# Exponentials of a score tile made per PSUM bank, and the product with V in bank order

## The chip, the cores and the metric

The kernel runs on one core of one Trainium2 chip. The time is that of one execution on the device, in microseconds (us); the median of several runs is compared. The engines are TensorE (PE in the profile, its weight loads PEld), VectorE (DVE), ScalarE (ACT), GpSimd (POOL) and SyncE (SP), which issues most transfers.

## The reference

A batch of 32 sequences of 128 tokens with 144 channels passes three transformer layers and then a rotation. Each layer is: normalise, modulate with a shift and a scale that come from a condition, attention with 16 heads of 9 channels, add; normalise, modulate, a multilayer perceptron (dense in layers 0 and 2, four experts with the best two chosen in layer 1), add. All in float32. The part that matters here is attention:

```python
scores = jnp.einsum('blhd,bmhd->bhlm', q * scale, k)
attn = jax.nn.softmax(scores, axis=-1)
o = jnp.einsum('bhlm,bmhd->blhd', attn, v).reshape(b, l, c)
return o @ W_proj + b_proj
```

The rotation at the end projects on 64 directions and applies a matrix exponential per sequence; its preparation runs on GpSimd, and in layer 1 on TensorE between other work (L1549).

## The kernel before

Each engine has its own instruction stream, written out by hand; they meet only through semaphores. A stream is in program order, so what stands where in the code is what the engine does next. Three layers follow each other, each with an attention stage and a perceptron stage. The attention stage is software-pipelined over pairs of sequences: the function `pair(i)` exists once per engine and interleaves steps of pairs i + 2 to i - 2.

For each sequence `b` there are two halves `a` of eight heads each. A half goes like this:

- `scores` on TensorE (L1375 and L1382). The product is made twice: with queries on the rows into `PSA`, from which VectorE takes the row maxima (L529), and with keys on the rows into `PSB`, with the maximum already subtracted. `PSA` and `PSB` are each two PSUM banks of 128x512 float32. Bank `r` of `PSB` is `PS[2 + r]` and holds four heads, one for each group `g` of 0 to 3.
- `exps` on ScalarE (L1070): one exponential over both banks of `PSB`, 128x1024, into `PT` in SBUF. `PT` is a part of the tensor BIG, so the profile writes BIG<-PSB. It adds 1 to the semaphore `exp_done`.
- `pv` on TensorE (L1399): eight products of `VA` (values of a head, and a column of ones that gives the sum of the row) with `PT`, into the one bank `PS[6]`. Each product writes 32 partitions, `p0 = HP * (2 * (g % 2) + r)` with HP = 32. The start partition decides which of the four 32-column tiles of the array works, so g and r pick the tile. A float32 product that isn't a transpose stands as two MATMUL and two LDWEIGHTS records in the trace.
- `out_copy` on ScalarE (L1076) copies `PS[6]` out, TensorE turns it back (`out_back`, L1419), VectorE divides by the sums (L541, L546), TensorE turns it again (`out_turn`, L1424 and L1425), and `project` (L1429, L1430) multiplies with the output weights.

Other names in the rows: `qk_turned` (L1360) transposes Q and K, and `qk_copy` on ScalarE (L1060) brings them to SBUF; `qkv_high` (L1046, L1047) and `qk_double` (L1053) prepare them; `max_turn` (L1411) transposes the maxima and `max_row` on VectorE (L537) adds them to Q; `h_modulate` (L1019, L1021) and `h_high` (L1033, L1034) prepare the normalised input; `split_product` (L1318) is the projection to Q, K, V and the first product of the perceptron, L1573 its second one.

The order around the change is set by hand in `pair`: ScalarE has for each pair `exps` for the odd sequence of the pair before (a = 1, then a = 0) and for the even one of this pair; TensorE takes the `pv` of these a half pair to a pair later. `scores` for the next half waits until `exps` has read `PSB`, by the same semaphore.

Of the kernel before, what the change touches and what calls it, by code (L numbers as in the profile page):

```python
# [8 lines left out]
ACT = mybir.ActivationFunctionType  # L9
AX = mybir.AxisListType  # L10

NB, T, C = 32, 128, 144
NH, HD = 16, 9
# [5 lines left out]
G, HG, HP = 4, 4, 32  # L19
# [28 lines left out]
def wait(eng, sem, value):  # L48

    if isinstance(value, int) and value <= 0:  # L50
        return
    eng.wait_ge(sem, value)
# [7 lines left out]
def program(nc, d, out, gates_dram, skew_dram):  # L60
    ctx = ExitStack()
    with ctx:
        def sb(name, shape, dt=F32):
            return ctx.enter_context(nc.sbuf_tensor(name, shape, dt))

        def sem(name):
            return ctx.enter_context(nc.semaphore(name))
# [22 lines left out]
        b2 = sb("b2", [128, NE, C])  # L90
# [18 lines left out]
        PT = BIG[:, 0:4096].rearrange("p (b a n) -> p b a n", b=2, a=2)  # L109
# [45 lines left out]
        PSA, PSB = (ctx.enter_context(nc.psum_tensor(f"PS{n}", [128, 1024], F32)) for n in ("A", "B"))  # L155
        PS = [PSA[:, 0:512], PSA[:, 512:1024], PSB[:, 0:512], PSB[:, 512:1024]]
# [21 lines left out]
        s2_done, exp_done = sem("s2_done"), sem("exp_done")  # L178
# [46 lines left out]
        def n_unit(l):  # L225
            return sum(EXPERTS[:l]) * NM
# [729 lines left out]
        def _(act):  # L956
            S = nc.scalar
# [52 lines left out]
            def attention(l):  # L1010
# [52 lines left out]
                def exps(b, u, a):  # L1063
                    act.wait_ge(s2_done, 2 * (NB * l + b) + 2 - a)
                    if b == 0:
                        wait(act, f2_done, n_unit(l) * MT)
                    if l == 1 and b == 0:
                        act.wait_ge(sk_st, 64)
                    wait(act, pv_done, NB * l + b - 1)
                    S.activation(PT[:, u % 2, a, :], PSB[:, :], ACT.Exp, scale=float(HD) ** -0.5).then_inc(exp_done, 1)  # L1070

                def out_copy(b, u):
                    n = NB * l + b
# [11 lines left out]
                def pair(i, gelus=None, high=None, rest=None):  # L1085
# [14 lines left out]
                    if last:  # L1100
                        exps(o - 2, o % 2, 1)
# [11 lines left out]
                    if last:  # L1113
                        exps(o - 2, o % 2, 0)
# [9 lines left out]
                    if at(0):  # L1124
                        exps(e, e % 2, 1)
# [142 lines left out]
        def _(pe):  # L1268
# [52 lines left out]
            def attention(l):  # L1321
# [42 lines left out]
                def scores(b1, b2, a):  # L1364

                    if b1 is not None:
                        wait(pe, max_done, 2 * (NB * l + b1) + a)
                    if b2 is not None:
                        pe.wait_ge(mrow, NB * l + b2 + 1)
                        wait(pe, exp_done, 2 * (NB * l + b2) + a)  # L1370
                    for g in range(G):
                        for r in range(2):
                            if b1 is not None:
                                rows, q0, par = slice(HP * (2 * a + r), HP * (2 * a + r + 1)), (b1 % 2) * 128, b1 // 2 % 2
                                one = mm(PS[r][:, g * 128:(g + 1) * 128], Q[rows, par, g, q0:q0 + 128],  # L1375
                                         KK[rows, par, g, q0:q0 + 128], start=True, stop=True)
                                if g == G - 1 and r == 1:
                                    one.then_inc(s1_done, 1)
                            if b2 is not None:
                                c = 1 - a  # L1380
                                rows, q0, par = slice(HP * (2 * c + r), HP * (2 * c + r + 1)), (b2 % 2) * 128, b2 // 2 % 2
                                two = mm(PS[2 + r][:, g * 128:(g + 1) * 128], KK[rows, par, g, q0:q0 + 128],  # L1382
                                         Q[rows, par, g, q0:q0 + 128], start=True, stop=True)
                                if g == G - 1 and r == 1:
                                    two.then_inc(s2_done, 1)

                def pv(b, u, a):

                    n = NB * l + b
                    if n == 0:  # L1390
                        pe.wait_ge(s_gev, 1)
                    if a == 1:
                        wait(pe, ot_ev, n)
                        pe.wait_ge(v_ev, n + 1)
                    pe.wait_ge(exp_done, 2 * n + 2 - a)
                    for g in range(G):
                        for r in range(2):
                            p0, at = HP * (2 * (g % 2) + r), (2 * a + g // 2) * 128
                            last = mm(PS[6][p0:p0 + HP, at:at + 128], VA[:, u, G * g + 2 * a + r, :],  # L1399
                                      PT[:, u % 2, a, (G * r + g) * 128:(G * r + g + 1) * 128], start=True, stop=True)  # L1400
                    if a == 0:
                        last.then_inc(pv_done, 1)
# [29 lines left out]
                def pair(i, first=None, turn_rows=None):  # L1432
# [7 lines left out]
                    if at(1):  # L1440
                        pv(e - 2, (e - 2) % 4, 1)
                    if at(2):
                        out_turn(e - 4, e % 2)
                    if now:
                        pe.wait_ge(qk_rd, 4 * (NP * l + i) + 2)
                    scores(e if now else None, o - 2 if before else None, 0)
                    if at(1):
                        pv(e - 2, (e - 2) % 4, 0)
# [8 lines left out]
                    if now:  # L1457
                        qk_turned(i, 3)
                    scores(e if now else None, o - 2 if before else None, 1)
                    if at(-1):  # L1460
                        qkv_product(i + 1, 0)
# [4 lines left out]
                    if before:  # L1466
                        pv(o - 2, (o - 2) % 4, 1)
# [9 lines left out]
                    if now:  # L1477
                        pe.wait_ge(qk_rd, 4 * (NP * l + i + 1))
                        scores(o, e, 0)
# [446 lines left out]
```

## Time and profile before

| | |
|---|---|
| median of three runs | 1349.75 us |
| lowest, highest | 1345.43, 1353.05 us |
| the profiled execution | 1347.33 us |
| its span, first to last instruction | 1345.5 us |
| granted TensorE clock, mean | 0.975 of full |
| TensorE busy | 1233.1 us, 92% |
| VectorE busy | 916.0 us, 68% |
| ScalarE busy | 820.6 us, 61% |
| the exponential (L1070) | 192 times, 196.4 us |
| the product with V (L1399) | 3072 records, 124.6 us |

Busy times are averages over stages of different kinds. The idle time of an engine costs something only where another waits for it. Attention takes the stretches 58 to 268, 386 to 600 and 988 to 1198 us.

### The profile page before, as it was taken

The page shows a single profiled execution, that of the slowest core. Times are in us where ns is not written, and L with a number is a line of the kernel's source. Part 1 is how long each engine was busy: PE and PEld are TensorE (multiplying, and loading weights), DVE is VectorE, ACT ScalarE, POOL GpSimd, SP SyncE. Part 2 cuts the span into 40 slices and gives each one's busy share as a digit, 9 for nine tenths or more (in the row PEclk, how much of TensorE's full clock was granted, in tenths as well). Part 3 has the DMA queues.
Part 4 walks back from the last instruction along what each step waited for, and adds up shares of the span by engine and source line. Part 5 has one row for each costly group of instructions (what it writes and reads, how often), then busy time and mean ns, then how long its engine had stood idle before and what let it go on. Part 6 is the DMA issues. An engine that isn't in the chain of part 4 may idle for free.

```text
span 1345.5 us, 36500 instructions
## 1 busy us (share of the span) xinstructions
PE 1233.1 (92%) x13322; PEld 1008.0 (75%) x13322; DVE 916.0 (68%) x2500; ACT 820.6 (61%) x1807; POOL 746.2 (55%) x2221
## 2 busy tenths in 40 slices
PE   2899999869989999988998999999879999979997
PEld 1677777658767777767887888888757777758775
DVE  6788888656568989875556545645489989865422
ACT  2598888736568888883322332332368888865541
POOL 4656565665656665656667666777777776000000
PEclk9999999979989999998999999999989999999997
DMA  6221212333251212141111111110011110011120
GB/s 161 41 18 16 21 18 19 44 94 36 37 123 15 16 19 17 17 67 15 13 6 13 15 13 7 34 37 15 19 39 29 32 31 13 13 18 26 19 62 27
DMA packets 50135, 42.90 MB, mean 32 GB/s; under 512 B 8266, under 2 KB 45565, under 8 KB 49528
## 3 DMA queue, kind: packets, MB, share of 16 engines
q1 hardware_dynamic: 45695, 29.91, 9.9%
q0 software_dynamic: 3488, 8.52, 9.0%
q8 instruction: 108, 1.77, 0.5%
q10 hardware_dynamic: 780, 2.17, 0.5%
q14 instruction: 64, 0.52, 0.1%
HBM read 33.86 MB, written 3.03 MB: 27 GB/s over the span
## 4 chain that ended last, share of the span: by engine, by line
PE 78%; DVE 15%; issue 4%; ACT 2%; DMA 1%; SPq 1%; DVEq 0%; ACTq 0%
PE PS L1573 17%; PE PSA L1318 14%; PE PS L1399 7%; PE PSA L1375 7%; PE PS L1318 6%; PE PS L1360 5%; PE PS L1411 3%; PE PS L1419 3%; DVE BIG L529 3%; DVE Q L537 2%; PE PS L1429 2%; PE PSB L1549 2%; PE PS L1430 2%; PE PSB L1318 1%; PE PSB L1382 1%
## 5 line engine op out<-in xcount | busy, mean ns | idle before, releaser
L1183 ACT ACTIVATE BIG<-PSA 128x512 f32<-128x512 f32 (+1 forms) x224 | 132.0, 593 | 302.1 <-PE PSA L1318 302.0
L1573 PE MATMUL PS<-w,BIG 128*128 128x144 f32 (+1 forms) x1920 | 257.2, 289 | 13.4 <-DVE BIG L766 5.9
L1573 PEld LDWEIGHTS PS<-w,BIG 128*128 128x128 f32 (+1 forms) x1920 | 247.2, 191 | 21.7 <-issue 7.3
L529 DVE TENSOR_REDUCE BIG<-PSA 128x8 f32<-128x1024 f32 x192 | 234.6, 1222 | 29.7 <-PE PSA L1375 28.1
L1070 ACT ACTIVATE BIG<-PSB 128x1024 f32<-128x1024 f32 x192 | 196.4, 1023 | 26.6 <-PE PSB L1382 25.6
L1375 PEld LDWEIGHTS PSA<-KK,Q 32*128 32x128 f32 x1536 | 105.3, 189 | 69.5 <-issue 48.7
L1375 PE MATMUL PSA<-KK,Q 32*128 32x128 f32 x1536 | 129.9, 285 | 28.4 <-DVE Q L537 15.6
L1382 PE MATMUL PSB<-Q,KK 32*128 32x128 f32 x1536 | 128.5, 285 | 0.0
L1360 PE MATMUL PS<-K,qt 128*128 128x128 f32 x768 | 121.5, 284 | 7.2 <-issue 3.1
L1399 PE MATMUL PS<-BIG,VA 128*32 128x128 f32 x3072 | 124.6, 280 | 1.6 <-DVE col L404 1.6
L1771 POOL MEMSET qprod<- 128x2 f32 x63 | 6.0, 96 | 208.5 <-DMA VB<-QA 208.5
L1753 POOL TENSOR_TENSOR qtree<-qtree 128x36 f32<-128x36 f32 (+3 forms) x384 | 103.4, 269 | 30.1
L770 DVE SCALAR_TENSOR_TENSOR BIG<-PS,BIG 128x144 f32<-128x144 f32 x96 | 34.7, 366 | 109.3 <-PE PS L1573 108.8
L1360 PEld LDWEIGHTS PS<-K,qt 128*128 128x128 f32 x768 | 89.9, 144 | 21.7 <-issue 13.2
L1318 PE MATMUL PSA<-hhi,Mhi 128*128 128x512 f32 (+1 forms) x224 | 101.8, 455 | 4.6 <-issue 3.6
L1382 PEld LDWEIGHTS PSB<-Q,KK 32*128 32x128 f32 x1536 | 101.4, 187 | 1.1 <-DVE Q L537 0.6
L1758 POOL TENSOR_TENSOR qtree<-qtree 128x4 f32<-128x4 f32 (+3 forms) x384 | 83.0, 216 | 30.0
L1399 PEld LDWEIGHTS PS<-BIG,VA 128*32 128x32 f32 x3072 | 72.6, 109 | 25.3 <-issue 16.4
L1318 PE MATMUL PSA<-hhi,Mlo 128*128 128x512 f32 (+1 forms) x224 | 90.4, 404 | 0.0
L1318 PE MATMUL PSA<-h,MW 128*128 128x512 f32 (+1 forms) x224 | 90.0, 402 | 0.0
L1318 PE MATMUL PSA<-hlo,Mhi 128*128 128x512 f32 (+1 forms) x224 | 89.8, 401 | 0.0
L537 DVE TENSOR_TENSOR Q<-Q,PS 128x512 fp32r<-128x512 f32 x96 | 65.9, 686 | 33.2 <-PE PS L1411 28.4
(287 smaller groups left out, 3089.5 us busy)
## 6 DMA issues: line engine op xcount, KB each, us to landing
gate<-gates SPq DMA_DIRECT2D x96, 72.0 KB, 2.9
mgate<-gates SPq DMA_DIRECT2D x96, 72.0 KB, 2.7
VB<-skew POOLq DMA_DIRECT2D x16, 288.0 KB, 3.7
X<-in_x SPq DMA_DIRECT2D x4, 576.0 KB, 14.5
out<-X SPq DMA_DIRECT2D x8, 288.0 KB, 4.1
BIG<-in_skew_w SPq DMA_DIRECT2D x2, 1024.0 KB
w<-in_w SPq DMA_DIRECT2D x1, 1440.0 KB, 9.9
BIG<-in_wqkv SPq DMA_DIRECT2D x2, 584.0 KB
```

Source lines behind the costliest of these rows:

```text
L529: V.tensor_reduce(nmax[:, :, 3 * HD + 2 * HP * a:3 * HD + 2 * HP * a + HP + 1:HP].rearrange("p g r -> p r g"), PSA[:, :].rearrange("p (r g ...
L537: V.tensor_tensor(q, q.bitcast(F32), PS[5][:, :].rearrange("p (g n) -> p g n", g=G), ALU.add).then_inc(mrow, 1)
L1070: S.activation(PT[:, u % 2, a, :], PSB[:, :], ACT.Exp, scale=float(HD) ** -0.5).then_inc(exp_done, 1)
L1183: S.activation(hm[0:rows, slot, :], PS[(par * FTOT[l] + j) % 2][0:rows, :], gelu).then_inc(gelu_done, 1)
L1318: last = mm(o, a, b, start=(k == 0), stop=(k == 3))
L1360: last = nc.tensor.transpose(turn_bank(pn, j)[:, g * 128:(g + 1) * 128], qt[:, s, j % 2, 4 * g:4 * g + 4, :].rearrange("p h w -> p (h w)") ...
L1375: one = mm(PS[r][:, g * 128:(g + 1) * 128], Q[rows, par, g, q0:q0 + 128], KK[rows, par, g, q0:q0 + 128], start=True, stop=True)
L1382: two = mm(PS[2 + r][:, g * 128:(g + 1) * 128], KK[rows, par, g, q0:q0 + 128], Q[rows, par, g, q0:q0 + 128], start=True, stop=True)
L1399: last = mm(PS[6][p0:p0 + HP, at:at + 128], VA[:, u, G * g + 2 * a + r, :], PT[:, u % 2, a, (G * r + g) * 128:(G * r + g + 1) * 128], star ...
L1573: last = mm(o, hm[0:rows, slot, s * 128:(s + 1) * 128], w2[0:rows, FT * e + k, :], start=(k == 0), stop=(k == FT - 1))
L1753: link(R.tensor_tensor(t[:, 0:n, :], a[:, :, 0:half], a[:, :, half:2 * half], ALU.add))
L1758: link(R.tensor_tensor(t[:, 0:n, :], a[:, :, 0:half], a[:, :, half:2 * half], ALU.add))
```

## The change

`exps` makes two exponentials of 128x512, one for each bank of `PSB`, and each adds 1 to `exp_done`. Everything that waits for that semaphore counts in twos. In `pv` the loops are exchanged: bank `r` is the outer one and group `g` the inner one, and each bank's four products wait for that bank's exponential.

```diff
@@ exps, ScalarE
-                    S.activation(PT[:, u % 2, a, :], PSB[:, :], ACT.Exp, scale=float(HD) ** -0.5).then_inc(exp_done, 1)
+                    for r in range(2):
+                        S.activation(PT[:, u % 2, a, 512 * r:512 * r + 512], PS[2 + r][:, :], ACT.Exp, scale=float(HD) ** -0.5)\
+                            .then_inc(exp_done, 1)
@@ scores, TensorE
-                        wait(pe, exp_done, 2 * (NB * l + b2) + a)
+                        wait(pe, exp_done, 2 * (2 * (NB * l + b2) + a))
@@ pv, TensorE
-                    pe.wait_ge(exp_done, 2 * n + 2 - a)
-                    for g in range(G):
-                        for r in range(2):
+                    for r in range(2):
+                        pe.wait_ge(exp_done, 2 * (2 * n + 1 - a) + r + 1)
+                        for g in range(G):
                             p0, at = HP * (2 * (g % 2) + r), (2 * a + g // 2) * 128
                             last = mm(PS[6][p0:p0 + HP, at:at + 128], VA[:, u, G * g + 2 * a + r, :],
                                       PT[:, u % 2, a, (G * r + g) * 128:(G * r + g + 1) * 128], start=True, stop=True)
```

On TensorE, in the second pair of layer 0, around the product of the odd sequence. Before (L1411 is `max_turn`, L1399 `pv`, L1424 and L1425 `out_turn`):

```order
L1411 MATMUL PS<-K,BIG 128x128 [waits hf_ready,max_done]
L1411 MATMUL PS<-K,BIG 128x128 x3
L1399 MATMUL PS<-BIG,VA 32x128 [waits exp_done,v_ready,ot_copied]
L1399 MATMUL PS<-BIG,VA 32x128 x7
L1424 MATMUL PS<-K,BIG 128x128 [waits o_normalised]
L1425 MATMUL PS<-K,BIG 17x128
```

The same place after the change, where the lines have moved down by two:

```order
L1413 MATMUL PS<-K,BIG 128x128 [waits hf_ready,max_done]
L1413 MATMUL PS<-K,BIG 128x128 x3
L1401 MATMUL PS<-BIG,VA 32x128 [waits exp_done,v_ready,ot_copied]
L1401 MATMUL PS<-BIG,VA 32x128 x3
L1401 MATMUL PS<-BIG,VA 32x128 [waits exp_done]
L1401 MATMUL PS<-BIG,VA 32x128 x3
L1426 MATMUL PS<-K,BIG 128x128 [waits o_normalised]
L1427 MATMUL PS<-K,BIG 17x128
```

The neighbours stand where they stood. The eight products now have a wait in their middle, and the four on either side of it write two 32-partition tiles only: 0 and 2 ahead of the wait, 1 and 3 behind it, where the eight went 0, 1, 2, 3, 0, 1, 2, 3.

On ScalarE, in the same pair, before (L1060 is `qk_copy`, L1076 `out_copy`, L1046, L1047 and L1053 prepare Q, K and V of the next pair):

```order
L1070 ACTIVATE BIG<-PSB 128x1024 [waits pv_done,s2_done]
L1060 ACTIVATE Q<-PS 128x4x128 [waits s2_done,qk_turned]
L1076 ACTIVATE BIG<-PS 128x512 [waits o_back,pv_done]
L1060 ACTIVATE KK<-PS 128x4x128 [waits s2_done,qk_turned]
L1046 ACTIVATE qt<-PS 128x32x9 [waits qk_turned,qkv_product]
L1047 ACTIVATE VA<-PS 128x16x9
L1053 ACTIVATE qt<-qt 128x2x16x9 [waits qk_high]
L1070 ACTIVATE BIG<-PSB 128x1024 [waits pv_done,s2_done]
```

After:

```order
L1071 ACTIVATE BIG<-PSB 128x512 [waits pv_done,s2_done]
L1071 ACTIVATE BIG<-PSB 128x512
L1060 ACTIVATE Q<-PS 128x4x128 [waits s2_done,qk_turned]
L1078 ACTIVATE BIG<-PS 128x512 [waits o_back,pv_done]
L1060 ACTIVATE KK<-PS 128x4x128 [waits s2_done,qk_turned]
L1046 ACTIVATE qt<-PS 128x32x9 [waits qk_turned,qkv_product]
L1047 ACTIVATE VA<-PS 128x16x9
L1053 ACTIVATE qt<-qt 128x2x16x9 [waits qk_high]
L1071 ACTIVATE BIG<-PSB 128x512 [waits pv_done,s2_done]
L1071 ACTIVATE BIG<-PSB 128x512
```

Each exponential has become two that stand next to each other; the first keeps the waits, and nothing else has moved.

## Rows read from the trace of the kernel before

**Rows 1.** The page: busy times by engine, and the clock in 40 slices.
```profile
PE 1233.1 (92%) x13322; PEld 1008.0 (75%) x13322; DVE 916.0 (68%) x2500; ACT 820.6 (61%) x1807; POOL 746.2 (55%) x2221
...
PEclk9999999979989999998999999999989999999997
```

**Rows 2.** The page: the chain that ended last, by engine and by line.
```profile
PE 78%; DVE 15%; issue 4%; ACT 2%; DMA 1%; SPq 1%; DVEq 0%; ACTq 0%
PE PS L1573 17%; PE PSA L1318 14%; PE PS L1399 7%; PE PSA L1375 7%; PE PS L1318 6%; PE PS L1360 5%; PE PS L1411 3%; PE PS L1419 3%; DVE BIG L529 3%; DVE Q L537 2%; PE PS L1429 2%; PE PSB L1549 2%; PE PS L1430 2%; PE PSB L1318 1%; PE PSB L1382 1%
```

**Rows 3.** Windows of the three attention stages: length, then busy us, PE, PEld, DVE, ACT, POOL.
```profile
58.00:268.00 210.00, 200.60 (x2842) 160.31 (x2838) 180.41 (x448) 180.21 (x403) 129.84 (x368) 0.99 0.22 22
386.00:600.00 214.00, 201.29 (x2844) 160.39 (x2844) 183.23 (x440) 184.93 (x408) 133.05 (x377) 0.98 0.21 21
988.00:1197.90 209.90, 199.93 (x2869) 159.43 (x2869) 181.87 (x442) 183.30 (x410) 116.52 (x381) 1.00 0.11 23
```

**Rows 4.** Waits, 58 to 268 us: who waited for whom, us, times, longest.
```profile
ACT qt L1046 <- PE PS L1318: 13.2, 14, 1.1
ACT BIG L1070 <- PE PSB L1382: 9.2, 17, 2.0
...
PE PSA L1375 <- DVE Q L537: 5.2, 15, 0.7
```

**Rows 5.** Line 1070, the exponential: its duration, and who waited for it.
```profile
L1070 ACT ACTIVATE BIG<-PSB x192: 996/1024/1034, 51.1 to 1193.2; 128x1024 f32<-128x1024 f32 x192
...
who waited for it (us, times):
PE PSA L1375: 2.8, 3
```

**Rows 6.** Timeline of TensorE from 207.4 us: start, length, line.
```profile
207.49 0.64 PE L1399 MATMUL PS<-BIG,VA 128*32 128x128 f32 x16
208.06 0.66 PE L1411 MATMUL PS<-K,BIG 128*128 128x128 f32 x4
```

**Rows 7.** Windows from 207.48: L1399 matmul records begun (the number behind x).
```profile
207.48:207.52 0.04, 0.03 (x4) 1.00 0.00 0
...
207.48:207.65 0.17, 0.16 (x8) 1.00 0.00 0
...
207.48:207.76 0.28, 0.27 (x12) 1.00 0.00 0
...
207.48:207.87 0.39, 0.38 (x16) 1.00 0.00 0
```

**Rows 8.** Windows from 659.60: L1549 weight loads begun.
```profile
659.60:659.71 0.11, 0.10 (x4) 1.00 0.00 0
659.60:659.73 0.13, 0.12 (x6) 1.00 0.00 0
```

**Rows 9.** Windows from 659.60: L1549 matmuls begun.
```profile
659.60:659.73 0.13, 0.12 (x4) 1.00 0.00 0
659.60:659.77 0.17, 0.16 (x4) 1.00 0.00 0
```

**Rows 10.** Timeline of ScalarE: start, length, line.
```profile
204.65 0.60 ACT L1060 ACTIVATE Q<-PS 128x512 fp32r<-128x512 f32 x1
205.14 0.59 ACT L1076 ACTIVATE BIG<-PS 128x512 f32<-128x512 f32 x1
205.62 0.60 ACT L1060 ACTIVATE KK<-PS 128x512 fp32r<-128x512 f32 x1
...
213.87 1.02 ACT L1070 ACTIVATE BIG<-PSB 128x1024 f32<-128x1024 f32 x1
214.77 0.45 ACT L1046 ACTIVATE qt<-PS 128x288 fp32r<-128x288 f32 x1
```

**Rows 11.** Groups by form, weight loads: busy us, mean ns; idle before them.
```profile
L1399 PEld LDWEIGHTS PS<-BIG,VA 128*32 128x32 f32 x3072 | 72.6, 109 | 25.3 <-issue 16.4 <-DVE col L404 1.8
...
L1419 PEld LDWEIGHTS PS<-K,BIG 128*128 128x128 f32 x384 | 43.5, 140 | 13.0 <-issue 9.5
```

## The prediction, made before the changed kernel had run

> **What bounds the kernel now.** I read the page's busy line first: TensorE is busy for 1233.1 us of the 1345.5 us span, ScalarE for 820.6 [rows 1]. The chain that ended last is 78% TensorE, 15% VectorE, 2% ScalarE, and the product with V (L1399) is among its larger entries at 7% [rows 2]. The change lies in the attention stages only, so I then cut the trace into them: in 58 to 268 us TensorE is busy for 200.60 of 210.00 us and ScalarE for 180.21; the other two attention stages look alike [rows 3]. So TensorE sets the pace there, and ScalarE has 27 to 30 us of idle time per stage. The waits of the first stage say what that idle time is: ScalarE waits for TensorE (13.2 us before L1046, 9.2 us before the exponential), while TensorE waits for VectorE (5.2 us) or for nothing that the trace shows [rows 4].
>
> Then the two places of the change. Who waits for the exponential: one group alone, the scores of L1375, three times, 2.8 us in all. The product with V never does [rows 5]. And how the product runs: one group of it is eight products, seen as 16 matmul records (two per product); it begins at 207.49 us and the next work begins at 208.06, 0.57 us later [rows 6].
>
> **The change, part by part.**
>
> *Earlier start of the product.* The first half of a product could now start when the first bank's exponential is done, about half a microsecond sooner. Nobody waits at that point [rows 5], so I take 0. The upper bound for a gain: 16.4 us of unexplained idle time stand before the weight loads of L1399 [rows 11]; were all of it a hidden wait for an exponential, the gain would be 16.4 us. Against it: the transposes of L1419, which read no exponential, have 9.5 us of the same kind before them [rows 11].
>
> *Two exponentials for one.* There are 192 of them, of 1024 ns each [rows 5]. Of a half I have no row, but a copy of the same 128x512 shape from PSUM to SBUF on the same engine: back to back, L1060, L1076 and L1060 start at 204.65, 205.14 and 205.62, so one costs 0.48 to 0.49 us of the engine's time. The whole exponential costs 0.90 us from its start at 213.87 to the next start at 214.77 [rows 10]. Two halves: 0.97 us, so 0.07 us more, times 192 = 13.4 us on ScalarE. ScalarE has 27 us or more idle per stage of 64 exponentials, whose share is 4.5 us, and it is not named as a releaser of TensorE in the first stage's large waits [rows 3, 4]. Cover: the idle time before L1046 and before the exponential itself, which comes in every pair of batches. Bounds: 0 on the path, or all 13.4 us if the cover is gone. I take 1 us, since the chain holds 2% of ScalarE only [rows 2]. What stands behind a later second half on ScalarE are the copies of Q and K and of the output; the scores wait for those.
>
> The Trainium skill (ScalarE: Activation LUTs, What ACT_TABLE_LOAD costs) gives an ACTIVATE a fixed 186 ns beside 0.833 ns per column, with about 93 ns of it overlapped back to back. By that a split would add about 93 ns, 17.9 us in all; the rows above have 0.07 us, and the sum goes by them.
>
> *The order of the product.* This is the part that I think decides. The eight products go to four column tiles of 32 output partitions. Before, neighbours in the program go to tiles 0, 1, 2, 3, 0, 1, 2, 3. After, the first half (r = 0) goes to 0, 2, 0, 2 and the second to 1, 3, 1, 3. Today the four tiles work at the same time: counting records that have begun since 207.48, there are 4 at 0.04 us, 8 at 0.17, 12 at 0.28, 16 at 0.39; four rounds of four, 0.11 us apart [rows 7]. Does the second half still find tiles 1 and 3 in parallel with 0 and 2? That hangs on how far TensorE lets an instruction pass one that waits for its own tile. Some passing is already there: each product is two records on one tile, and yet the first round holds four tiles, so the second record of a product was passed by the next product. One more row goes further. The 64x64 products of L1549 alternate between two tiles, two records each. At 0.13 us after their start, six weight loads have begun but only four matmuls [rows 8, 9]. The sixth load is the third one of the second tile, and in program order both records of the first tile's second product stand ahead of it, neither of whose matmuls had begun. So at least two pieces of work may wait at one tile while later work for the other goes on. The new order needs three to wait at tile 0 (record two of the first product, and both of the second). I found no row with three.
>
> If three may wait, the second half follows the first at the pace at which a round is handed out: four records begin within 0.04 us [rows 7], so tiles 1 and 3 begin some 0.015 to 0.02 us later than now, and so does the end: 192 x 0.015 = 3 us. That lies on the path, since TensorE is the chain. If only two may wait, the second half begins with the second round, 0.13 us late: 192 x 0.13 = 25 us. If the second half begins only after the first has been handed on entirely, four more rounds: 192 x 0.44 = 84.5 us. I take the first: the row nearest in kind shows passing with every slot filled that it can test, and nothing held up.
>
> *The waits.* TensorE gets one more wait in each group, in its middle, for an exponential that is by then done; 0, since nobody waits for L1070 here. The first wait's value and that of the scores are the same points in time as before.
>
> **Sum.** 3 us for the order, 1 us for ScalarE, 0 for the start: +4 us. The profiled execution took 1347.33 us, which gives 1351.3; it stands 2.4 us under the median of the three runs, 1349.75, so on the median the sum gives 1353.8, called 1354: slower by 0.3%, which a measurement cannot tell from no change (about 0.5%, 6.7 us).
>
> **Rivals.**
> - *A, the forecast:* all four tiles still overlap and ScalarE's extra is covered: 1350 to 1360. Chance 0.59.
> - *B, a short queue at each tile:* two pieces may wait, the third blocks. 25 us for the order and 1 us for ScalarE: 1376. For it: two is all that L1549 proves. Against: queues that are exactly as long as the evidence would be a coincidence. Chance 0.14.
> - *C, two tiles at a time:* the second half waits for the first. The products go two by two, eight rounds in place of four, 84.5 + 1 us: 1435. It decides as soon as later work cannot pass a product whose tile is taken. Against it: such passing was seen [rows 8, 9]. The wait in the middle could still make a boundary that today's groups don't have. Chance 0.12. The Trainium skill (TensorE: Matmul & The Clock Gate, The mechanism) says that matmuls start and end in strict program order and only weight loads are pulled ahead, with neighbours on different tiles overlapping. With a product as the unit, that is this rival; taken record by record, today's four starts within 0.04 us could not be, so the trace does not bear it out in full.
> - *D, ScalarE is late:* the 13.4 us land on the path, by the copies of Q and K behind the exponentials: 3 + 13.4: 1366. Busy for 180 of 210 us, it has little room in single pairs. Against: no wait of TensorE for it. Chance 0.11.
> - *E, a faster kernel:* the idle time before L1399 was a wait for the exponential after all: 1349.75 - 16.4 + 4 = 1337. Chance 0.04.
>
> **How the numbers follow.** The likeliest case is A; its own range is 1347 to 1360. The range for all: B and D lie above A, C is left out (0.12) with E (0.04); so 1345 to 1380. Faster by over 0.5%: E and a sliver of A, 0.05. Slower by over 0.5%: B, C, D, 0.37, and the upper end of A (above 1356.5), 0.05: 0.42. Same: 0.53.
>
> **What would show it.** In the profile after: the group of 16 records is followed by the next work after 0.59 us (A), 0.70 (B) or 1.01 (C), where it is 0.57 now [rows 6]; records begun count 4, 8, 12, 16 within about 0.4 us (A) or 2 by 2 up to 0.8 us (C). The exponential's 384 halves last about 0.59 us each and start 0.48 to 0.49 us apart, ScalarE's busy time grows by about 13 us, and TensorE's waits for it stay near 3 us; if they grow above 10 us it is D. The clock should stay as it is, granted in full in nearly all slices [rows 1]. The prediction is wrong above all if three records cannot wait at one tile.

## The result, and the profile after

The changed kernel takes 1353.01 us (median), the kernel before it 1349.28 us in the same session; the ratio is 1.0028, with a 95% interval of 1.0015 to 1.0041. That is 2.0 to 5.5 us more, about 3.8 us. The forecast was 4 us more. A second measurement, on another occasion (below), gave 1.0027.

The page of the changed kernel, busy times and chain, which answer to [rows 1, 2] (lines have moved down by two behind the change):

```profile
PE 1241.9 (92%) x13322; PEld 1018.9 (75%) x13322; DVE 917.8 (68%) x2500; ACT 829.6 (61%) x1999; POOL 748.3 (55%) x2221
...
PE 79%; DVE 14%; issue 4%; ACT 2%; DMA 1%; SPq 1%; DVEq 0%; ACTq 0%
```

ScalarE has 192 instructions more and 9.0 us more busy time. TensorE still holds most of the chain. The profiled execution itself took 1355.18 us, where that of before took 1347.33; single executions of one kernel lie up to 10 us apart here (1349.27 to 1358.02 for this one), so the two spans can't be subtracted to find 4 us. Something smaller has to be read.

Line 1071, the halved exponential, answering to [rows 5]:

```profile
L1071 ACT ACTIVATE BIG<-PSB x384: 566/597/614, 53.6 to 1202.9; 128x512 f32<-128x512 f32 x192
...
who waited for it (us, times):
PE PSA L1377: 0.8, 3
```

A half takes 597 ns where the whole took 1024. As before, nobody waits for an exponential but the scores at three places; the product with V (L1401) is not in the list, so its earlier start bought nothing. What the pair costs ScalarE stands in the timeline (start, length), at a place like the one in [rows 10], where the next instruction follows at once:

```profile
504.69 1.07 ACT L1071 ACTIVATE BIG<-PSB 128x512 f32<-128x512 f32 x2
505.64 0.45 ACT L1046 ACTIVATE qt<-PS 128x288 fp32r<-128x288 f32 x1
```

Start to next start is 0.95 us for the two halves, where the whole took 0.90: 0.05 us more. Such places are about a quarter of all; what happens at the others is told with the exponential in four and eight pieces.

Now the product. Windows of the changed kernel from 505.66 us, matmul records of L1401 begun; the group begins at 505.67:

```profile
505.66:505.68 0.02, 0.01 (x2) 1.00 0.31 29
505.66:505.69 0.03, 0.02 (x2) 1.00 0.41 39
505.66:505.70 0.04, 0.03 (x4) 1.00 0.51 58
```

The same place of the kernel before, one pair's product in the same layer, which begins at 498.97:

```profile
498.96:498.98 0.02, 0.01 (x2) 1.00 0.71 86
498.96:498.99 0.03, 0.02 (x3) 1.00 0.68 77
498.96:499.00 0.04, 0.03 (x4) 1.00 0.67 72
```

Before, the first round's four tiles begin one after the other without a gap. After, two begin, then for a moment nobody, then the other two: tiles 1 and 3 stand behind eight and ten records in the program, where they stood behind two and six. All four still begin within 0.04 us, long before the first round ends (0.13 us). At the trace's full resolution, finer than the rows, the median starts in a group are 0, 7, 13 and 20 ns before and 0, 7, 27 and 33 ns after; the next work, counted from its first weight load, begins after 573 ns before and 586 ns after. So tile 1 begins 20 ns later than it did, and tile 3, the last one, 13 ns. The groups then run on in rounds of four as in [rows 7]. The end moves with the last tile: 13 ns a group, 192 times, 2.5 us.

That this lands on the path is seen where nothing else disturbs the attention stage. Starts of the product of the odd sequence, one pair of sequences apart, in the timeline of TensorE. Before:

```profile
485.87 0.64 PE L1399 MATMUL PS<-BIG,VA 128*32 128x128 f32 x16
...
512.08 0.64 PE L1399 MATMUL PS<-BIG,VA 128*32 128x128 f32 x16
```

After:

```profile
492.52 0.33 PE L1401 MATMUL PS<-BIG,VA 128*32 128x128 f32 x4
...
518.82 0.66 PE L1401 MATMUL PS<-BIG,VA 128*32 128x128 f32 x16
```

Two pairs take 26.21 us before and 26.30 us after. They hold eight groups: 0.09 / 8 = 0.011 us each, with rows that are rounded to 0.01 us.

### The profile page after: what moved, and what is told of

Its sections match the earlier page's. It is cut to its first block, busy times and chain, and to the rows that moved or that the text cites. A ratio compares the mean times of both kernels' runs of the same rounds, so it can differ in the third digit from the quotient of the medians.

```text
span 1353.4 us, 36692 instructions
## 1 busy us (share of the span) xinstructions
PE 1241.9 (92%) x13322; PEld 1018.9 (75%) x13322; DVE 917.8 (68%) x2500; ACT 829.6 (61%) x1999; POOL 748.3 (55%) x2221
## 4 chain that ended last, share of the span: by engine, by line
PE 79%; DVE 14%; issue 4%; ACT 2%; DMA 1%; SPq 1%; DVEq 0%; ACTq 0%
PE PS L1575 17%; PE PSA L1320 14%; PE PS L1401 7%; PE PSA L1377 7%; PE PS L1320 6%; PE PS L1362 5%; PE PS L1413 4%; PE PS L1421 3%; DVE Q L537 2%; DVE BIG L529 2%; PE PS L1431 2%; PE PSB L1551 2%; PE PS L1432 2%; PE PSB L1320 1%; PE PSB L1384 1%
## 5 line engine op out<-in xcount | busy, mean ns | idle before, releaser
L1071 ACT ACTIVATE BIG<-PSB 128x512 f32<-128x512 f32 x384 | 207.5, 596 | 27.9 <-PE PSB L1384 27.4
L1401 PE MATMUL PS<-BIG,VA 128*32 128x128 f32 x3072 | 128.3, 282 | 1.1 <-DVE col L404 1.1
L1362 PEld LDWEIGHTS PS<-K,qt 128*128 128x128 f32 x768 | 91.7, 146 | 20.7 <-issue 13.6
L1401 PEld LDWEIGHTS PS<-BIG,VA 128*32 128x32 f32 x3072 | 76.0, 110 | 25.4 <-issue 16.9
```

What stands on the lines that cost most here:

```text
L1071: S.activation(PT[:, u % 2, a, 512 * r:512 * r + 512], PS[2 + r][:, :], ACT.Exp, scale=float(HD) ** -0.5)\
L1362: last = nc.tensor.transpose(turn_bank(pn, j)[:, g * 128:(g + 1) * 128], qt[:, s, j % 2, 4 * g:4 * g + 4, :].rearrange("p h w -> p (h w)") ...
```

## The experiments

Theory 1: the loss is the later start of two of the four tiles. Theory 2: it is ScalarE's longer exponentials. Other questions were what the wait in the middle costs, and how many records may wait at one tile, on which the three large branches of the prediction hung. The ratios below are to the kernel before, run beside each.

**The exponentials alone.**

```diff
-S.activation(PT[:, u % 2, a, :], PSB[:, :], ACT.Exp, ...).then_inc(exp_done, 1)
+for r in range(2):
+    last = S.activation(PT[:, u % 2, a, 512 * r:512 * r + 512], PS[2 + r][:, :], ACT.Exp, ...)
+last.then_inc(exp_done, 1)
```

> The exponential in two halves, the product with V as before (tiles 0, 1, 2, 3 in turn, one wait for both halves). Theory 1 (the small loss comes from the order of the product, 0.013 us a group): 0 to 1 us over the kernel before, ScalarE busy about 9 us more. Theory 2 (it comes from ScalarE's longer exponentials): 3 to 4 us over it, the whole of what the change costs.

1348.85 us beside 1348.54; ratio 1.0002 (0.9987 to 1.0018), so 0.3 us, between -1.8 and 2.4. ScalarE is busy for 829.1 us, 8.5 us more than before. That excludes theory 2's 3 to 4 us.

**The order alone.**

```diff
-for g in range(G):
-    for r in range(2):
+for r in range(2):
+    for g in range(G):
```

> One exponential as before, the eight products in the order of banks (tiles 0, 2, 0, 2, 1, 3, 1, 3), one wait ahead. Theory 1: the group's next work begins 0.586 us after its start where it was 0.573, 192 times, so 2.5 us over the kernel before. Theory 2: no difference. If the wait in the middle were what delays tiles 1 and 3, the group would take 0.573 us here.

1350.55 us beside 1348.54; ratio 1.0004 (0.9990 to 1.0018), so 0.5 us, between -1.3 and 2.4. (The two medians lie 2.0 us apart, more than the ratio gives; both are inside that interval.) In the trace the median starts are 0, 7, 27 and 33 ns, and the next work begins after 586 ns: exactly the changed kernel's, without any wait in the middle. The interval ends just short of theory 1's 2.5 us, so the time alone neither shows it nor quite holds it. The pairs do. Two pairs, from the timeline of the order alone:

```profile
486.53 0.66 PE L1399 MATMUL PS<-BIG,VA 128*32 128x128 f32 x16
...
512.85 0.33 PE L1399 MATMUL PS<-BIG,VA 128*32 128x128 f32 x4
```

And of the split alone:

```profile
484.46 0.32 PE L1401 MATMUL PS<-BIG,VA 128*32 128x128 f32 x4
...
510.68 0.32 PE L1401 MATMUL PS<-BIG,VA 128*32 128x128 f32 x4
```

26.32 us with the order alone, as in the changed kernel (26.30); 26.22 with the split alone, as before (26.21).

Two places could be chance, so here are all three layers. Taken is the time from one product group to the fourth after it, which is one pair of sequences, 60 times a layer; since other things lengthen many of these times, the lower quartile (a quarter of them are shorter) is the steadier figure. It is worked out from the starts in the traces:

| kernel | lower quartile in layers 0, 1, 2, us | median, us |
|---|---|---|
| before | 13.11, 13.11, 13.11 | 13.11, 13.11, 13.12 |
| split alone | 13.11, 13.11, 13.11 | 13.12, 13.15, 13.11 |
| order alone | 13.14, 13.15, 13.15 | 13.15, 13.16, 13.16 |
| both (the change) | 13.16, 13.15, 13.15 | 13.17, 13.15, 13.16 |

So the steady part of the loss belongs to the order: 0.04 to 0.05 us a pair, 48 pairs, 2 to 2.4 us. The split alone leaves the steady pair as it was.

**One wait in place of two.** The changed kernel, with the wait for both halves ahead of the eight products.

```diff
-for r in range(2):
-    pe.wait_ge(exp_done, 2 * (2 * n + 1 - a) + r + 1)
+pe.wait_ge(exp_done, 2 * (2 * n + 1 - a) + 2)
+for r in range(2):
```

> The changed kernel with one wait for both halves ahead of the eight products, in place of the wait in their middle. If the wait costs nothing: the same starts within the group (0, 7, 27, 33 ns) and the time of the changed kernel, 3 to 4 us over the kernel before. If it costs: less than that, by its price.

1351.48 us beside 1347.66; ratio 1.0028 (1.0012 to 1.0044), the same as the changed kernel's. The starts in a group are 0, 7, 27 and 33 ns and the next work begins after 586 ns, also the same. A wait that is already met, in the middle of a group, costs nothing that can be measured.

**The changed kernel again**, beside the one above.

> The changed kernel again, beside the one above: 3 to 4 us over the kernel before, if the sum of both parts holds (the split alone gave 0.3 us, the order alone 0.5 us, each with an uncertainty of about 2 us).

1351.03 us beside 1347.66; ratio 1.0027 (1.0012 to 1.0042), so 3.6 us, between 1.6 and 5.7.

**The exponential in four, and in eight pieces.**

```diff
-S.activation(PT[:, u % 2, a, :], PSB[:, :], ACT.Exp, ...).then_inc(exp_done, 1)
+for r in range(4):
+    last = S.activation(PT[:, u % 2, a, 256 * r:256 * r + 256], PSB[:, 256 * r:256 * r + 256], ACT.Exp, ...)
+last.then_inc(exp_done, 1)
```

> The exponential in four pieces of 128x256, the product as before. Each piece more costs ScalarE about 0.07 us, so 0.2 us an exponential and 40 us in all. Theory 1, with ScalarE covered: under 5 us over the kernel before. Theory 2: ScalarE is near the path and a good part shows, 15 to 40 us.

1351.02 us beside 1348.54; ratio 1.0021 (1.0006 to 1.0036), so 2.8 us, between 0.8 and 4.9. From the timeline of ScalarE, an exponential and what follows:

```profile
210.52 1.21 ACT L1071 ACTIVATE BIG<-PSB 128x256 f32<-128x256 f32 x4
211.58 0.33 ACT L1084 ACTIVATE BIG<-PS 128x128 f32<-128x128 f32 x1
```

1.06 us from start to next start. Where L1046 follows, as in [rows 10], it is 1.05 us, 0.15 more than with the whole one. But the next instruction does not follow at once everywhere. Ahead of the copies of Q and K (L1060) the kernel before and the one with four pieces show:

```profile
210.44 1.03 ACT L1070 ACTIVATE BIG<-PSB 128x1024 f32<-128x1024 f32 x1 [0.43 <-PE PSB L1382]
211.53 0.60 ACT L1060 ACTIVATE KK<-PS 128x512 fp32r<-128x512 f32 x1
```

```profile
206.09 1.18 ACT L1071 ACTIVATE BIG<-PSB 128x256 f32<-128x256 f32 x4
207.18 0.60 ACT L1060 ACTIVATE Q<-PS 128x512 fp32r<-128x512 f32 x1
```

The copy begins 1.09 us after the start of the exponential, in one piece or in four; why it does not begin sooner behind the whole one isn't shown. Copies of Q or K follow 93 of the 192 exponentials. So the extra of one place times 192 is too much. The page gives the sum: ScalarE's busy time is 836.1 us, 15.5 more than before.

> The exponential in eight pieces of 128x128, the product as before. ScalarE's extra is seven times 0.07 us or more for each of 64 exponentials, over 30 us in each attention stage, where it had 27 to 30 us idle. Here the cover should be used up: 10 to 40 us over the kernel before, and waits of TensorE for ScalarE in the trace. Under 5 us would say that ScalarE has still more room.

1360.93 us beside 1347.66, from four executions; ratio 1.0101 (1.0065 to 1.0137), so 13.6 us, between 8.8 and 18.5. The timeline and the waits:

```profile
207.46 1.43 ACT L1071 ACTIVATE BIG<-PSB 128x128 f32<-128x128 f32 x8
208.72 0.50 ACT L1046 ACTIVATE qt<-PS 128x288 fp32r<-128x288 f32 x1
```

```profile
PE PSA L1377 <- ACT BIG L1071: 17.4, 47, 0.7
```

1.26 us, 0.36 more than the whole one, and now the copies of Q and K are late too. ScalarE is busy for 870.4 us, 49.8 more than before. TensorE waits for the exponential 47 times, 17.4 us, where it had been 2.8 before and was 1.9 with four pieces. The lower quartile of a pair, as in the table above, is 13.11, 13.11 and 13.10 us with four pieces, as before, and 13.31, 13.30 and 13.30 with eight: 0.2 us a pair, 9 us in 48 pairs. So ScalarE's extra is covered in the steady pair up to four pieces and no longer with eight. The idle time that [rows 3] add up to, some 85 us, is no measure of that cover: with eight pieces ScalarE is still idle for 58 us of the three stages (windows some 16 us longer in all), and TensorE waits nevertheless. The 2.8 us of the four pieces stand nowhere in the steady pair; where they come from is open.

**Tile by tile.** One exponential; four records of one tile in a row.

```diff
-for g in range(G):
-    for r in range(2):
+for r in range(2):
+    for g in (0, 2, 1, 3):
```

> One exponential, the order of products tile by tile: 0, 0, 2, 2, 1, 1, 3, 3, so that four records of a tile stand in a row. If work is handed to the tiles at 0.0034 us a record and three may wait at a tile: the tiles begin at 0, 0.014, 0.027 and 0.041 us, the next work begins 0.594 us after the group's start, 4 us over the kernel before. If only two may wait at a tile: the last tile begins after 0.13 to 0.4 us and the kernel is 25 to 75 us slower.

1350.74 us beside 1348.54; ratio 1.0016 (0.9998 to 1.0034), so 2.2 us, between -0.3 and 4.6. Windows from 217.36, where a group begins, records begun:

```profile
217.36:217.37 0.01, 0.01 (x1) 1.00 0.18 58
217.36:217.38 0.02, 0.02 (x2) 1.00 0.21 58
217.36:217.40 0.04, 0.04 (x3) 1.00 0.30 87
217.36:217.41 0.05, 0.05 (x4) 1.00 0.71 256
```

The four tiles begin at 0, 13, 27 and 40 ns and still overlap; the second record of the first tile begins at 133 ns, and the next work after 592 ns. Three records wait at tile 0 while the other tiles begin, nine at three tiles when the last one begins, and nothing is held up. The lower quartile of a pair is 13.17 us in each layer, 0.06 more than before, 2.9 us in all.

**How long a row of one tile may be.** Here the products are made twice or four times, each overwriting its own result, so the times are those of more work. The two orders tile by tile, twice and four times, each have a control with the tiles in turn. Each of these times is that of one execution; the differences are far larger than the 10 us by which executions of one kernel differ.

```diff
+for g, r in [(g, r) for g in range(G) for r in range(2)] * 2:                          # twice, in turn
+for g, r in [(g, r) for r in range(2) for p in range(2) for g in (p, p + 2) * 2]:      # twice, by tile
```

> Control. Every product with V is made twice (the second overwrites the first with the same numbers), tiles 0, 1, 2, 3 in turn: eight rounds of four records, 0.11 us apart, the tiles begin 0.007 us apart and the next work starts 1.01 us after the group's start.

> The same doubled products, tile by tile, so that eight records of one tile stand in a row. If the tiles' queues hold that much: the tiles begin at 0, 0.027, 0.054 and 0.082 us, the group takes 0.06 us more than the control in turn. If a tile holds fewer than seven waiting records: the later tiles begin one or more rounds (0.11 us each) later, and the group grows by that for each tile.

In turn 1418.81 us, by tile 1679.61, beside 1350.29 for the kernel before. The same 32 records take from start to next start 1.01 us in turn and 2.39 us by tile. Timelines, in turn and by tile:

```profile
207.14 1.08 PE L1399 MATMUL PS<-BIG,VA 128*32 128x128 f32 x32
208.15 0.66 PE L1419 MATMUL PS<-K,BIG 128*128 128x128 f32 x4
```

```profile
225.25 2.46 PE L1399 MATMUL PS<-BIG,VA 128*32 128x128 f32 x32
227.64 0.44 PE L1360 MATMUL PS<-K,qt 128*128 128x128 f32 x2
```

Windows by tile, from 225.24: the second tile begins only between 0.46 and 0.48 us.

```profile
225.24:225.61 0.37, 0.36 (x4) 1.00 2.15 116
225.24:225.70 0.46, 0.45 (x4) 1.00 2.27 123
225.24:225.72 0.48, 0.47 (x6) 1.00 2.42 130
```

Four records have begun one by one, all on the first tile; then the fifth and the first of the next tile come together. When the fifth begins, records six to eight wait: three. Since nine could wait at three tiles in the run tile by tile above, the limit belongs to the single tile and isn't one on everything that waits.

> Control. Every product four times, tiles in turn: sixteen rounds, the next work 1.89 us after the group's start.

> The same fourfold products, tile by tile: sixteen records of one tile in a row. With queues without an end the tiles begin at 0, 0.054, 0.109 and 0.163 us. I expect an end somewhere here: later tiles begin several rounds late, and the number of rounds tells how many records may wait.

1582.82 us in turn, 2348.66 us by tile. Windows by tile, from 304.75:

```profile
304.75:306.07 1.32, 1.32 (x12) 1.00 0.00 0
304.75:306.09 1.34, 1.34 (x13) 1.00 0.00 0
304.75:306.10 1.35, 1.35 (x14) 1.00 0.00 0
```

Twelve records one by one, and with the thirteenth the next tile: again three wait (fourteen to sixteen). From these two I put a number on six in a row ahead of its run.

```diff
+for g, r in [(g, r) for r in range(2) for p in range(2) for g in (p, p + 2, p)]:       # twelve products
```

> Twelve products a group, tile by tile with three products (six records) each. In the run with eight records in a row the second tile began with the first tile's fifth record, in the run with sixteen with the thirteenth: each time three records were still waiting. If three is the number, the second tile begins here with the third record of the first, 0.25 us after the group's start, the third at 0.50, the fourth at 0.75, and the next work at about 1.53 us, near 184 us over the kernel before. If six fit (a queue counted in some other way), the tiles begin at 0, 0.020, 0.041 and 0.061 us and the group takes 0.85 us, about 53 us over the kernel before.

```profile
225.40:225.54 0.14, 0.14 (x2) 1.00 0.00 0
225.40:225.65 0.25, 0.25 (x3) 1.00 0.00 0
225.40:225.66 0.26, 0.26 (x4) 1.00 0.00 0
```

The next tile begins with the third record, 0.25 us after the start, and the next work after 1.52 us; 1513.79 us beside 1348.42, 165 us more, a little less than the 184 forecast. A part of the difference goes into waits that were there: in the attention stages TensorE's idle time falls from 31 us to 22. So three records may wait at a tile behind the one that runs; the fourth holds up everything behind it.

## Why the prediction was right

*What bounds.* TensorE's chain, with ScalarE covered, held: of the 0.013 us a group, most came through (0.04 to 0.05 us in a pair of four groups) where nothing else disturbed a pair.

*Earlier start: 0.* Held. The product never waited for an exponential, before or after. The unexplained gaps of [rows 11] are still there, 16.9 us of them before the weight loads of L1401, and the kernel isn't faster; with that rival E is gone.

*Two exponentials for one: 13.4 us on ScalarE, 1 us on the path.* The price was too high: 0.05 us rather than 0.07 where the next instruction follows at once, and nearly nothing at many of the other places, so that busy time grew by 9.0 us (8.5 with the split alone) and not by 13. The 93 ns worked out from the Trainium skill (ScalarE: Activation LUTs, What ACT_TABLE_LOAD costs) were further off. On the path the split alone measured 0.3 us (-1.8 to 2.4), which neither shows nor excludes the 1 us; the steady pair shows 0. Rival D's 13.4 is excluded. With eight pieces the cover gives out, so the covering was real and has an end, though the idle time per stage, on which the prediction leaned, doesn't tell where.

*The order: 3 us.* Measured 13 ns a group, 2.5 us; the trace shows the mechanism as written: tiles 1 and 3 begin 0.020 and 0.013 us late, and the end moves by 0.013. The count of what may wait was the open point, and "three may wait" turned out true with nothing to spare: three is the limit. The rows had shown only two, so the choice of three was partly luck. Rival B was one record away; what happens past the limit is seen in the run with six in a row. Rival C is excluded: the halves overlap in every group. The rule named with it, that matmuls start in strict program order (the Trainium skill, TensorE: Matmul & The Clock Gate, The mechanism), does not hold here: in the tile-by-tile run four tiles begin within 0.05 us while the first tile's second record waits until 0.13.

*The waits: 0.* Held, by the run with one wait.

*Sum.* 4 us forecast, 3.8 (2.0 to 5.5) and 3.6 (1.6 to 5.7) measured. That the two agree to a few tenths is luck, as the intervals say. The parts measured alone add to 0.8 us with an uncertainty of about 3, and the traces give 2 to 2.5 us for the order. So that much of the loss is shown. Where the remaining 1.3 us or so come from is open: they are smaller than what these runs can resolve, and the steady pair of the split alone doesn't bear out that they are ScalarE's.

## What to carry to other kernels

Splitting a stage for an earlier start pays only where somebody waits at that point: the list of who waits for the instruction says so before any work is done. Where small float32 products go to four column tiles, let four successive products go to all four of them. Two tiles first and then the other two costs 13 ns a group of eight, two products in a row on one tile cost 20 ns, and a third in a row costs whole rounds of 0.11 us. And an engine that is off the path takes a bit more work almost for nothing, up to a point that its idle time doesn't tell: here 8.5 and 15.5 us of extra busy time left the steady pair as it was and cost 0.3 and 2.8 us in all, each uncertain by about 2, while 49.8 us made every pair 0.2 us longer and cost 13.6.

## What the runs showed of the hardware

- At a 128x32 tile of the array, one record (a weight load with its matmul) runs and three wait; a fourth stops all that is behind it in the program, also work for idle tiles. Rows of 4, 6, 8 and 16 records: the next tile began with the first, third, fifth and thirteenth record (0.01, 0.25, 0.47 and 1.34 us after the start). The limit is one of each tile: nine records waited at three tiles without holding up the fourth.
- Work is handed to the tiles in program order at about 3.3 ns a record: behind four records in a row on a tile the next tile begins after 13 ns, behind twelve after 40.
- A record of a product with 128 columns keeps its tile for 0.11 us (0.13 the first of a group). Eight products on four tiles in turn take 0.57 us with what surrounds them; sixteen take 1.01 us in turn and 2.39 us tile by tile, twelve tile by tile 1.52 us (in turn an estimated 0.79, halfway between 0.57 and 1.01).
- A wait that is already met costs nothing measurable between two products.
- Exponentials of one ScalarE stream that follow each other at once start 0.904, 0.478, 0.263 and 0.158 us apart for 1024, 512, 256 and 128 columns (medians; the halves start either 0.478 or 0.493 apart). That is 0.83 ns a column and 0.05 us for each instruction, worked out from these four; a cut of one instruction into two costs those 0.05 us.
